# Attention outputs of images one to three in six products of 128 rows instead of eight of 96, with gathers in eight, four and four

## What is computed

```python
value, query = dwconv(ln(x), w_v), dwconv(ln(x), w_q)      # stride 1
key, off = dwconv(ln(x), w_k, 2), dwconv(ln(x), w_off1, 2)  # 28 x 28 points
pos = tanh(einsum('bhwc,pc->bhwp', gelu(norm(off)), w_off2) + ref)
v_sampled = grid_sample_bilinear(value, pos)                # four corners of each point
attn = einsum('bcm,bcn->bmn', query, key) * SCALE           # 12 heads of 32 over quarters of the pixels
out = einsum('bmn,bcn->bcm', attn, v_sampled)
x = x + einsum('bchw,oc->bohw', out, w_out)
t = t + ffn(ln(t))          # four experts, the best two weighted; 96 -> 384 -> 96
x = x + large_conv(ln(x))   # 7x7, 5x3, 3x5 and separable kernels, depthwise
t = t + ffn(ln(t))
```

## Time and profile before

| | |
|---|---|
| median of three runs | 1598.78 us (1594.95 to 1599.26) |
| the profiled execution | 1595.69 us |
| its span, first to last instruction | 1593.8 us |
| mean granted clock of TensorE | 0.956 of full speed |
| TensorE busy with matmuls | 1430.9 us, 90% |
| VectorE busy | 1138.5 us, 71% |
| ScalarE busy | 726.6 us, 46% |
| GpSimd busy | 510.9 us, 32% |
| DMA moved | 136.55 MB, mean 86 GB/s |

### The profile page before, as it was taken

One profiled execution on the slowest core, in us unless ns is written; L12 is line 12 of the kernel. 1 busy time (PEld: TensorE's weight loads), 2 busy tenths in 40 slices (PEclk: granted clock), 3 DMA queues, 4 the chain that ended last, 5 costly groups with the idle time before them and its releaser, 6 DMA issues.

```text
span 1593.8 us, 21538 instructions
## 1 busy us (share of the span) xinstructions
PE 1430.9 (90%) x6736; PEld 1058.4 (66%) x6736; DVE 1138.5 (71%) x2881; ACT 726.6 (46%) x1508; POOL 510.9 (32%) x533
## 2 busy tenths in 40 slices
PE   6879687988788999998788999999999999998998
PEld 4656554555555676665455577787888788877786
DVE  6955987399974454369995544687878877699787
ACT  5622353245442444455543334454545544356544
POOL 4051143011540000001171000254445533465575
PEclk9988788998989999998999999999999999999999
DMA  5532234313424222332252322353234422221121
GB/s 122 134 114 60 52 93 108 117 57 101 111 65 126 56 76 70 84 117 67 70 142 69 105 70 55 80 128 96 65 89 104 103 67 61 73 82 58 54 70 57
DMA packets 168404, 136.55 MB, mean 86 GB/s; under 512 B 114785, under 2 KB 161923, under 8 KB 167907
## 3 DMA queue, kind: packets, MB, share of 16 engines
q1 hardware_dynamic: 163314, 129.91, 30.6%
q0 software_dynamic: 3072, 4.82, 1.3%
q10 hardware_dynamic: 1904, 0.43, 0.1%
HBM read 95.47 MB, written 39.30 MB: 85 GB/s over the span
## 4 chain that ended last, share of the span: by engine, by line
PE 50%; issue 12%; DVE 11%; POOL 7%; ACT 5%; DMA 1%; SPq 1%; ACTq 0%; POOLq 0%; DVEq 0%
PE at_ps L1349 10%; PE y_ps L1201 7%; PE h_ps L1208 5%; PE h_ps L1210 5%; PE h_ps L1209 5%; POOL pix_mem L1075 4%; PE y_ps L1190 4%; PE y_ps L1191 3%; PE y_ps L1192 3%; PE at_ps L1268 3%; DVE vq_mem L1554 2%; POOL ln_rstd L1048 2%; ACT ln_cen L868 2%; PE lb_ps L1163 2%; PE lg_ps L1176 1%
## 5 line engine op out<-in xcount | busy, mean ns | idle before, releaser
L1003 ACT ACTIVATE hidden<-h_ps,b 128x448 f32<-128x448 f32 x609 | 384.6, 634 | 619.5 <-PE h_ps L1210 606.5
L1208 PE MATMUL h_ps<-xh,w1h 96*128 96x448 f32 x672 | 367.1, 546 | 2.6 <-ACT hidden L1003 1.3
L1048 POOL TENSOR_TENSOR ln_rstd<-ln_ve,minus_half 112x4 f32<-112x4 f32 x112 | 154.7, 1381 | 661.2 <-DVE ln_ve L1493 655.0
L1201 PE MATMUL y_ps<-hidden,w 128*96 128x448 f32 x672 | 326.0, 570 | 14.3 <-ACT hidden L1003 13.9
L1510 DVE SCALAR_TENSOR_TENSOR part<-y_ps,b,gate_t 96x448 f32<-96x448 f32 x224 | 151.4, 676 | 207.0 <-PE y_ps L1201 170.5
L1067 POOL CAST in_w<-hidden 128x448 fp32r<-128x448 f32 x273 | 200.2, 737 | 243.6 <-ACT hidden L1003 162.4
L1209 PE MATMUL h_ps<-xl,w1h 96*128 96x448 f32 x672 | 250.1, 372 | 0.0
L1210 PE MATMUL h_ps<-xh,w1l 96*128 96x448 f32 x672 | 249.8, 372 | 0.0
L1208 PEld LDWEIGHTS h_ps<-xh,w1h 96*128 96x128 f32 x672 | 130.0, 193 | 90.7 <-issue 60.9
L1209 PEld LDWEIGHTS h_ps<-xl,w1h 96*128 96x128 f32 x672 | 131.5, 196 | 67.2 <-issue 61.8
L1554 DVE SCALAR_TENSOR_TENSOR vq_mem<-x_mem,all_w,vq_mem 128x770 f32<-128x770 f32 (+1 forms) x168 | 163.3, 1016 | 1.7 <-POOL ln_rstd L1048 0.7
(11 more groups left out here) (186 smaller groups left out, 2149.2 us busy)
## 6 DMA issues: line engine op xcount, KB each, us to landing
gate_t<-gates_dram SPq DMA_DIRECT2D x112, 336.0 KB, 3.3
value_pairs<-pix_mem SPq DMA_DIRECT2D x56, 168.0 KB, 3.2
x_mem<-norm_c SPq DMA_DIRECT2D x16, 420.0 KB, 4.3
x_mem<-norm_a SPq DMA_DIRECT2D x14, 336.0 KB, 3.7
res_mem<-in_x SPq DMA_DIRECT2D x4, 1176.0 KB, 11.3
x_attn<-res_mem SPq DMA_DIRECT2D x16, 294.0 KB, 2.7
res<-x_attn SPq DMA_DIRECT2D x28, 168.0 KB, 2.9
x_ffn<-ffn_out SPq DMA_DIRECT2D x28, 168.0 KB, 2.0
```

Of the source, the lines that this page charges most:

```text
L1003: act.activation(to[:, :], h_ps[c % H_BANKS][:, 0:TILE], ACT.Gelu, bias=b1[l][:, c:c + 1]).then_inc(gelu_done, 1)
L1048: pool.tensor_tensor(ln_rstd[n % 2][:, :], ln_ve[n % 2][:, :], minus_half[0:SUB, 0:NSUB], ALU.pow)\
L1201: pe.matmul(y_ps[e % Y_BANKS][0:C, 0:TILE], w2[l][:, c, :], hidden[c % HID_RING][:, :], start=(j == 0), stop=(j == CPE - 1)).then_inc(hid_ ...
L1208: pe.matmul(ps, hi, xh[:, ring(k)], start=True, stop=False)
```

## The change

Images one to three make their attention output in six products, one for each group of 128 of the 384 rows of quarter and channel and each half of the columns. The residual then lies in 128 partitions by 3 groups (`x_res_rows`) and is loaded and stored in six pieces (`runs`), each a run of channels of one quarter: (group, first row, last row, quarter, first channel) are (0, 0, 96, 0, 0), (0, 96, 128, 1, 0), (1, 0, 64, 1, 32), (1, 64, 128, 2, 0), (2, 0, 32, 2, 64) and (2, 32, 128, 3, 0). The gathers of these images are issued as 0 to 8 in stage 2 (image one) or 3, and 8 to 12 and 12 to 16 in stage 4. Row 1 is sampled ahead of `combine2` of stage 5. Image zero stays as it was.

```diff
+        x_res_rows = res_mem[:, 0:G * QPIX].rearrange("p (j n) -> p j n", j=G)
+        runs = []
+        for row in range(0, Q * C, 32):
+            j, r, q, o = row // 128, row % 128, row // C, row % C
+            if runs and runs[-1][0] == j and runs[-1][3] == q:
+                runs[-1][2] = r + 32
+            else:
+                runs.append([j, r, r + 32, q, o])
...
-        AT_USES = 2 + VBLK + 2 + 1 + G + 2 * Q
+        AT_USES = 2 + VBLK + 2 + 1 + G + 2 * G
+        ATTN_RUNS = [sum(run[3] == q for run in runs) for q in range(Q)]
+
+        def attn_stored(q, images):
+            return 16 * (min(images, 1) + ATTN_RUNS[q] * max(images - 1, 0))
...
             def store_attn(b, q):
-                sp.wait_ge(at_free, AT["attn", b] + AT_Y + 2 * (q + 1))
                 cols = slice(q * QPIX, (q + 1) * QPIX)
-                sp.dma_start(x_attn[b][:, cols], x_res[:, cols]).then_inc(attn_st[q], 16)
+                if b == 0:
+                    sp.wait_ge(at_free, AT["attn", b] + AT_Y + 2 * (q + 1))
+                    sp.dma_start(x_attn[b][:, cols], x_res[:, cols]).then_inc(attn_st[q], 16)
+                    return
+                for j, r0, r1, quarter, o in runs:
+                    if quarter == q:
+                        sp.wait_ge(at_free, AT["attn", b] + AT_Y + 2 * (j + 1))
+                        sp.dma_start(x_attn[b][o:o + r1 - r0, cols], x_res_rows[r0:r1, j, :]).then_inc(attn_st[q], 16)
...
-                    sp.dma_start(x_res[:, :], x_in[b]).then_inc(xres_ld, 16)
+                    if b == 0:
+                        sp.dma_start(x_res[:, :], x_in[b]).then_inc(xres_ld, 16)
+                    else:
+                        for j, r0, r1, q, o in runs:
+                            sp.dma_start(x_res_rows[r0:r1, j, :],
+                                         x_in[b][o:o + r1 - r0, q * QPIX:(q + 1) * QPIX]).then_inc(xres_ld, 16)
...
                 if 4 in stages and stages[4] > 0:
-                    gather(stages[4], 4, 8)
-                if 5 in stages and stages[5] > 0:
-                    gather(stages[5], 10, 14)
+                    gather(stages[4], 8, 12)
                 if 1 in jobs:
                     scale_rows(jobs[1])
...
                 if 2 in stages and stages[2] in ON_PE:
-                    gather(stages[2], 0, 4)
+                    gather(stages[2], 0, 4 if stages[2] == 0 else 8)
                 if 3 in stages and stages[3] == 0:
                     gather(0, 8, 12)
                 if 3 in stages and stages[3] not in ON_PE:
-                    gather(stages[3], 0, 4)
+                    gather(stages[3], 0, 8)
                 if 4 in stages and stages[4] > 0:
-                    gather(stages[4], 8, 10)
-                if 5 in stages and stages[5] > 0:
-                    gather(stages[5], 14, 2 * GQ)
+                    gather(stages[4], 12, 2 * GQ)
...
-                q, h = i // 2, i % 2
+                q, h, rows = i // 2, i % 2, C if b == 0 else 128
                 use(b, AT_Y + max(0, i - spare(b, AT_Y)))
                 for g in range(G):
-                    last = pe.matmul(at_bank(b, AT_Y + i)[0:C, 0:YCOL], m2[:, g, q * C:(q + 1) * C],
+                    last = pe.matmul(at_bank(b, AT_Y + i)[0:rows, 0:YCOL], m2[:, g, q * rows:(q + 1) * rows],
                                      query[:, g, h * YCOL:(h + 1) * YCOL], start=(g == 0), stop=(g == G - 1))
...
-                    elif b > 0 and Y_CHUNK <= c < Y_CHUNK + 2 * Q:
+                    elif b > 0 and Y_CHUNK <= c < Y_CHUNK + 2 * G:
                         times_query(b, c - Y_CHUNK)
-                        if c == CHUNKS - 1:
-                            times_query(b, 2 * Q - 2)
-                            times_query(b, 2 * Q - 1)
...
-                dve.tensor_tensor(x_res[:, cols], at_bank(b, AT_Y + i)[0:C, 0:YCOL], x_res[:, cols], ALU.add).then_inc(at_free, 1)
+                dve.tensor_tensor(res_mem[0:rows, cols], at_bank(b, AT_Y + i)[0:rows, 0:YCOL], res_mem[0:rows, cols],
+                                  ALU.add).then_inc(at_free, 1)
...
-            Y_BEFORE = {"normalize1": (0,), "combine2": (1, 2), "combine3": (3, 4, 5, 6), "end": (7,)}
+            Y_BEFORE = {"normalize1": (0,), "combine2": (1, 2), "combine3": (3, 4, 5)}
...
-                        if stage == 5 and name == "combine3":
+                        if stage == 5 and name == ("combine3" if b == 0 else "combine2"):
                             sample_row(b, 1)
```

More of the change, by code:

```diff
@@ L450, in metaformer_kernel @@
         at_size = {"attn": AT_USES, "gen": GEN, "conv": FILLS}
-        AT = {user: sum(at_size[kind] for kind, _ in at_order[:i]) for i, user in enumerate(at_order)}
+        AT = {user: sum(at_size[kind] + 2 * (Q - G) * ((kind, n) == ("attn", 0)) for kind, n in at_order[:i])
+              for i, user in enumerate(at_order)}
         O_STEPS, G_STEPS, VAL_STEPS = 19, 12, 6
@@ L608, in load_norm @@
                         for q in range(job.tile * TILE // QPIX, -(-(job.tile + 1) * TILE // QPIX)):
-                            sp.wait_ge(attn_st[q], 16 * (b + 1))
+                            sp.wait_ge(attn_st[q], attn_stored(q, b + 1))
                     else:
@@ L692, in load_acc @@
                         for q in range(Q):
-                            sp.wait_ge(attn_st[q], 16 * NB)
+                            sp.wait_ge(attn_st[q], attn_stored(q, NB))
                     if b >= 2:
@@ L779, in _ @@
                         if b > 0:
-                            sp.wait_ge(attn_st[q], 16 * b)
+                            sp.wait_ge(attn_st[q], attn_stored(q, b))
                     if b == 1:
@@ L1609, in add_y @@
                 if i == 0:
-                    dve.wait_ge(xres_ld, 16 * (b + 1))
+                    dve.wait_ge(xres_ld, 16 * (1 + len(runs) * b))
                 dve.wait_ge(at_full, AT["attn", b] + AT_Y + i + 1)
+                rows = C if b == 0 else 128
                 cols = slice(i * YCOL, (i + 1) * YCOL)
-                dve.tensor_tensor(x_res[:, cols], at_bank(b, AT_Y + i)[0:C, 0:YCOL], x_res[:, cols], ALU.add).then_inc(at_free, 1)
+                dve.tensor_tensor(res_mem[0:rows, cols], at_bank(b, AT_Y + i)[0:rows, 0:YCOL], res_mem[0:rows, cols],
+                                  ALU.add).then_inc(at_free, 1)
             def norm_off(b):
```

## The result

The changed kernel took 1571.35 us in the median (1567.82 to 1575.16), the kernel before 1596.89 on the same chips: ratio 0.984, interval 0.981 to 0.987, so 25.5 us less (20 to 31). The forecast was 1572.8. The profiled execution took 1575.16 us with a span of 1573.3, that is 20.5 less than the one before, where I had summed 26.0. So the profile, on which the sum was built, gained 5.5 us less than forecast, and the medians of the runs nearly as much as forecast: that the forecast of the time came out within 1.5 us is in part luck.

The account below looks back on a forecast made before the run. The prediction took TensorE's work and waits as the bound. It summed 16.7 for products and -0.5, +5.3, +4.4 for the three images' gathers to 26 us gained, forecasting 1572.8 us, range 1557 to 1587.

Parts of the forecast that it names:

- The products, 16.7 us: Attention outputs of images one to three: dropping products seven and eight with their waits saves 5.6 us an image.
- The waits before the product of keys and values, 26.9 us at most: TensorE's three waits for second-row sampling go, 18.8 us, plus 8.1 for the half-clock stretches after them.
- What GpSimd's queue takes back: Gathers moved ahead of normalization scales delay TensorE's turning back, leaving -0.5, +5.3 and +4.4 us for images one to three.
- Image one: Four gathers ahead of its scale: 7.0 us new wait plus 2.7 slow stretch, 9.7 lost against 9.2 won.
- the second bound: Image one's query taps on VectorE, shifted by 7.0, end at 274.7, 0.8 us after the first output product's old start.
- a scale that I had taken to be free: Images two and three: four gathers moved into stage 3 fit in 4.76 us of idle GpSimd before the scale.
- the turning back that I had priced at 2.7: Images two and three: six more gathers make a stage 4 scale 5.5 us late, of which 2.7 reach TensorE.
- The rival of moved waits: New waits at turning back eat all 26.9 us, leaving the products' 16.7 (1582 us) or down to 5; chance 0.17.
- an operation that reads PSUM: Gathers on GpSimd: beside anything on VectorE that reads PSUM, a gather takes 1 us.

Follow-up runs that it names:

- the third experiment: Image one's gathers as four in stage 2, four between stage 4's scales and eight after, against the changed kernel: 1559.6 us, ratio 0.977 to the kernel before.
- the fourth experiment: The changed kernel with the second row sampled ahead of the fourth expert's combination again: 1575.7 us, ratio 0.986 to the kernel before.
- the mended order: Image one's gathers in four; four and eight: 1559.6 us in the changed kernel, 1581.0 us with eight products kept.
- the second experiment: The kernel before with only gathers in eight, four, four and the second row sampled sooner, eight products kept: 1593.3 us, ratio 0.9985.
- the ninth experiment: Image one's gathers in four, four, eight, weights split later, images two and three's last eight gathers after stage 4's second scale: 1570.2 us, ratio 0.984.

## Why the prediction was right, and which term was not

**The products, 16.7 us: right.** Alone they were worth 17.3, and 5.4 in image one against 5.6. No cost of the wider weights is to be seen (a product without a wait takes 2.14 us in either form), nor one of the six loads of the residual (ratio 0.999).

**The waits before the product of keys and values, 26.9 us at most: right.** They and the slow stretches behind them are gone in all three images (clock 1.00, 1.50 to 1.52 us for the product).

**What GpSimd's queue takes back: the mechanism right, image one's size too small.** The sum took 17.7 us off 26.9 for it, 9.7 in image one and 4.0 in each of the others. The forecast for images two and three was 10.9 and 10.0 us, products included, and 12.0 and 9.0 were measured. For image one it was 5.1 and 0.1 was measured. The step that was mis-sized is "Image one": the sum took 7.0 us of new wait for the scale and one slow stretch, and measured were 8.1 (8.63 less the 0.56 of before), because two of the eight gathers took 3.69 and 4.11 us. And the second bound, that VectorE ends its query taps at 274.7, was shifted by 7.0 only. But VectorE waits for TensorE, so it is shifted by the slow stretch too: its combination that started at 229.86 started at 241.29, 11.4 us later, and the first output product at 278.08, 4.2 after where it had been. I saw this bound and took it for a confirmation, when it was the next term of the sum: 2.79 us of wait and 1.4 more for a product that then ran slow.

Image three's number hides a second error. I expected its loss in step (3, 1), where turning back has no wait at all in the changed kernel. Its wait is in (3, 0), 6.09 us where it had been 0.42, at a scale that I had taken to be free because its gathers would fit into the idle time ahead of it. In GpSimd's timeline the eighth gather ends at 794.98 and the scale behind it takes four times as long as a free one:

```profile
794.01 0.97 POOL L1100 DMA_INDIRECT pix_mem<-value_pairs,o_idx  x1 [0.30 <-issue]
795.01 4.44 POOL L1073 TENSOR_TENSOR ln_rstd<-ln_ve,minus_half 112x4 f32<-112x4 f32 x1
```

That the image's sum came out near the forecast is luck. Image two had waits of 1.42 us there and, in (1, 1), of 2.08 us before the turning back that I had priced at 2.7.

**That the scale behind the gathers is the cause** is shown by the third experiment: with the same sixteen gathers, all of them still issued in stage 4 or sooner, and the same sampling, only four fewer ahead of each scale of stage 4, the wait fell from 8.63 to 0.58 and the kernel gained some 11 us, image one 12.4. That order falls in the 9.8 us in which GpSimd had been idle ahead of stage 5's first scale.

**The early sampling** is a smaller part of the gain than the early gathers, some 3 us in the fourth experiment's profile: it is worth 5 us in images two and three and costs 1.8 in image one. Sampling late brings waits of 1.5 to 2.9 us, and sampling early holds a bank (3.10 us in image three).

**The rival of moved waits** was nearly true for the gathers' part by itself: 2 us alone. Together with the products the part was worth 8 (0.984 against 0.989), and with the mended order 20. So the two parts seem to give 6 us more together than apart, but the intervals of the three ratios are 3 to 5 us wide to either side, so this is not shown. In the profiled executions it is 1: in the steps of the three images the products won 17.2 us alone, the gathers 2.8 and the whole change 21.1. Timing alone moves such sums: the same order shows a first wait of 1.4 us in image two and 6.1 in image three of the same execution, and single runs spread over 17 us in the second experiment.

## What to carry to other kernels

A queue in order is priced by what stands behind the moved piece, not by the piece: find the idle time that stood ahead of the next urgent instruction, and put the moved work there. When a wait is moved to an earlier place, shift every engine that depends on it by the whole loss, the slow clock included, before its old times are used as a bound. And where two engines fill each other's gaps, a mean is a poor price: take the times of neighbours that run beside the same work.

## What the runs showed of the hardware

A tenth of a microsecond between GpSimd and VectorE went with a gather four times as long. In the kernel before, GpSimd's timeline has in (0, 0):

```profile
218.88 1.05 POOL L1075 DMA_INDIRECT pix_mem<-value_pairs,o_idx  x1 [0.23 <-issue]
```

and VectorE's:

```profile
219.38 2.87 DVE L1554 SCALAR_TENSOR_TENSOR vq_mem<-x_mem,all_w,vq_mem 128x770 f32<-128x770 f32 x3
```

The taps start 0.50 us behind the gather, which takes 1.05. In the changed kernel the gather at 219.53 has these behind it after 0.40 us, in VectorE's timeline:

```profile
219.93 2.87 DVE L1572 SCALAR_TENSOR_TENSOR vq_mem<-x_mem,all_w,vq_mem 128x770 f32<-128x770 f32 x3
```

It takes 4.11 us, until 0.84 after the three taps. The thirteen traces say the same. I took every gather in the steps of images one to three beside a run of two or more taps. The 32 that such a run followed after 0 to 0.45 us all ended 0.84 us or more behind the run, and the 70 that it followed after 0.49 us or more all took 0.96 to 1.68 us; between 0.45 and 0.49 there are both. Why so small a difference decides was not tried.

The gather of 3.69 us, too, which began with such taps, ended 0.85 after them: a gather is mostly held for a whole run of VectorE's operations, not for one. That is no rule without exception. Of 109 gathers that began while such a run was going, 10 ended before it did or with it, one of them in the changed kernel beside three taps that began at 236.81 and ended at 239.69:

```profile
237.56 1.12 POOL L1100 DMA_INDIRECT pix_mem<-value_pairs,o_idx  x1 [0.31 <-issue]
```

It ended 0.85 us after the first of the three. Nor does an operation that reads PSUM always let a gather in, as the prediction had it. The longest, 5.83 us in the ninth experiment, went on past a combination (415.74 to 416.41) that stood between VectorE's taps. The power of 112 x 4 elements, 1.01 us when free, took 4.44 in image three beside the taps. TensorE's granted clock stood at 0.50 in the 6 us after the wait of 8.63 and at 1.00 in each stretch of 5.4 us after the product of keys and values, where TensorE had been busy.
